# First attention of a two-layer transformer: scores as split fp32r products, normalisation on ScalarE

## The chip, the core and the metric

The kernel runs on one core of a Trainium2 chip. The metric is the device time of one execution in microseconds; the table below gives the median of three runs. A core has TensorE (matmuls, PE in the profile, its weight loads PEld), VectorE (DVE), ScalarE (ACT), GpSimd (POOL) and SyncE (SP, here it only issues transfers). They run side by side and wait for each other by semaphores. Matmul results land in PSUM, eight banks of 512 fp32 columns.

## The reference

Four blocks on x of 4 batches x 512 tokens x 256, each behind a layer norm and added to x: an attention with 16 query and 8 key/value heads of width 128, a mixture of 16 experts, a second attention, and an MLP with ternary weights. The change touches the first attention alone, which is, cut to what matters:

```python
q = rms_norm(einsum('btd,ndh->btnh', x, q_kernel), q_norm_scale)      # 16 heads of 128
k = rms_norm(einsum('bsd,kdh->bskh', x, k_kernel), k_norm_scale)      # 8 heads: 2 query heads share one
v = einsum('bsd,kdh->bskh', x, v_kernel)
q, k = apply_rope(q, positions), apply_rope(k, positions)
mask = (j <= i) & (i - j < 128)                                       # window of 128 tokens
probs = softmax(where(mask, (q * 128**-0.5) @ k.T, -max), axis=-1)
x = x + einsum('btnh,nhd->btd', probs @ v, out_kernel)
```

## The kernel before

Tokens lie in tiles of 128 (4 per batch) and heads in 8 groups of two query heads with their key/value head. A **step** n of a batch is one tile and one group: 32 steps a batch, tile n // 8 outermost, group n % 8 inside. Because the window is 128 tokens, a tile of queries sees two tiles of keys: its own and the one before. In the first 8 steps of a batch (`alone`) there is no older tile.

Each engine has its own written-out `attention_step(b, n, new, old, following)`; batch 0 and batch 3 are unrolled, batches 1 and 2 are passes of a loop on every engine. Within a step an engine works on different stages of up to ten steps (m = n - lag), always in the order of the code; nothing is reordered. The stages and their lags:

- lag 0: PE projects q, q, k, v of the group as one product of 512 columns in high and low parts (six fp32r matmuls, `split_product`, lines 1410 to 1412) into bank 0 or 1; ACT squares (line 1165) and keeps v (1168); DVE reduces (788) and rotates (794, 797, 798); POOL makes the inverse root (526, 528) and adds the rotated halves (530).
- lag 1: DVE scales q and k (777).
- lag 2: PE transposes them into bank 2 (1482); ACT copies all three to `qkT` (1174) and signals `qkT_ready`.
- lag 3: PE computes the scores (1493, 1496) into bank 3 or 4: per head one fp32 product of 128 columns with the older tile's keys and one with its own. An fp32 product is two passes in the trace, so a step with both tiles shows eight at line 1496. Steps without an older tile add the causal mask by a bf16 matmul.
- lag 4: DVE merges older and own scores under the mask into one half of the bank (746) and takes the maximum (768); ACT exponentiates with a row sum (1190) into `prob`, a part of `yT`.
- lag 6: DVE inverts the sums (737) and multiplies the probabilities by them (752), which signals `normed`; PE transposes the result into bank 5 (1525).
- lag 7: ACT copies it (1150); POOL cuts it into the older tile's and the own tile's part (514, 516).
- lag 9: PE multiplies with v (two fp32 products, four passes, line 1454; in steps without an older tile one product, line 1450); ACT and DVE split the result into high and low part (1158, 759).
- lag 10: PE projects it out (six fp32r matmuls of 256 columns, lines 1410 to 1412, `wo`) into bank 7; DVE adds it to x after the eighth group (813).

The order of PE in a step is: attended (lag 9), projection (0), transposes of q and k (2), scores (3), output projection (10), transposes of the probabilities (6). The order of ACT is: copy of the transposed probabilities (7), copy of attended (9), Square and v (0), copy of q and k (2), Exp (4).

At n % 8 == 5 the next tile of x is turned: PE transposes it (`turn_tile`, 1430) into bank 2, the bank of the turned q and k, and therefore waits first for the `qkT_ready` of step n - 2 (line 1502). ACT copies the tile (`tile_keep`, 1123) and DVE makes its low part (`tile_low`, 693). PE wants it in the next step (line 1480). The wait of line 1502:

```python
                if new and (following or n // GROUPS < TT - 1) and n % GROUPS == 5:
                    pe.wait_ge(qkT_ready, k0 + n - 1)
                    turn_tile(b, n // GROUPS + 1)
```

Of the kernel before, what the change touches and what calls it, by code (L numbers as in the profile page):

```python
# [16 lines left out]
ALU = mybir.AluOpType  # L17
# [58 lines left out]
def build(nc, dram, out):  # L76
    with ExitStack() as ctx:
# [40 lines left out]
        qkT = sb("qkT", [P, K_RING, 3, P], where=part_a)  # L118
# [119 lines left out]
        qk_turned, qkT_ready = sem("qk_turned"), sem("qkT_ready")  # L238
# [396 lines left out]
        def _(dve):  # L635
# [92 lines left out]
            def attention_step(b, n, new, old, following):  # L728
# [10 lines left out]
                if valid(m):  # L739

                    k, s = k0 + m, m % 2
                    bank = ps[:, 3 + s, :].rearrange("p (h a f) -> p h a f", h=2, a=2)
                    dve.wait_ge(scored, k + 1)
                    if not alone(m):
                        V.memset(spare[:, 1:2], 0.0)
                        V.copy_predicated(bank[:, :, 1, :], older[:], bank[:, :, 0, :]).then_inc(merged, 1)
                m = n - 6
                if valid(m):

                    k, s = k0 + m, m % 2  # L750
                    dve.wait_ge(inv_ready, k + 1)
                    V.tensor_tensor(prob[:, m % PROB_RING], prob[:, m % PROB_RING],  # L752
                                    rsums[:, s, :].unsqueeze(2).to_broadcast((P, 2, P)), ALU.mult).then_inc(normed, 1)
# [8 lines left out]
                if valid(m):  # L762

                    k, s = k0 + m, m % 2
                    bank = ps[:, 3 + s, :].rearrange("p (h a f) -> p h a f", h=2, a=2)
                    if not alone(m):
                        dve.wait_ge(merged, b * OLDER_STEPS + with_older(m))
                    V.tensor_reduce(nmax[:, s, :], bank[:, :, 1, :], AX.X, ALU.max, negate=True).then_inc(max_ready, 1)  # L768
# [12 lines left out]
                if new:  # L781
# [10 lines left out]
                    if not old and g == 0 and t > 0:  # L792
# [6 lines left out]
                                    ).then_inc(roped, 1)  # L799
                if new and (following or t < TT - 1):  # L800
                    if g == 1:
                        if not old and t in (0, TT - 1):
                            dve.wait_ge(x_loaded[1 + t // (TT - 1)], 16)
                        tile_stats_of(b, t + 1)
                    if g == 3:
                        tile_apply(b, t + 1)
                    if g == 5:
                        tile_low(b, t + 1)
# [301 lines left out]
        def _(act):  # L1110
# [26 lines left out]
            def attention_step(b, n, new, old, following):  # L1137
# [32 lines left out]
                if valid(m):  # L1170
# [3 lines left out]
                    A(qkT[:, m % K_RING, :, :], ps[:, 2, 0:3 * P].rearrange("p (h f) -> p h f", h=3), ACT.Copy  # L1174
                      ).then_inc(qkT_ready, 1)
                if new and (following or t < TT - 1) and g == 5:
                    tile_keep(b, t + 1)
                m = n - 4
                if valid(m):
# [7 lines left out]
                    if old or m >= PROB_RING:  # L1187
                        act.wait_ge(prob_turned, k - PROB_RING + 1)
                    for h in range(2):
                        ins = A(prob[:, m % PROB_RING, h, :], ps[:, 3 + s, (2 * h + 1) * P:(2 * h + 2) * P], ACT.Exp,  # L1190
# [214 lines left out]
        def _(pe):  # L1405
# [29 lines left out]
            def attention_step(b, n, new, old, following):  # L1435
# [49 lines left out]
                if valid(m):  # L1485
# [6 lines left out]
                    if alone(m):  # L1492
                        MM(bank[:, :, 1, :], ident_b[:], causal[:], start=True, stop=False, skip_group_check=True)
                    for h in range(2):
                        for part in ((1,) if alone(m) else (0, 1)):
                            ins = MM(bank[:, h, part, :], qkT[:, m % K_RING, h, :],  # L1496
                                     qkT[:, (m if part else m - GROUPS) % K_RING, 2, :],
                                     start=not alone(m) and h == 0 and part == 0,
                                     stop=h == 1 and part == 1, skip_group_check=True)
# [450 lines left out]
```

## Time and profile before

| | |
|---|---|
| median of 3 runs (lowest to highest) | 1417.8 us (1417.02 to 1418.81) |
| profiled execution | 1424.85 us |
| its span, first to last instruction | 1423.1 us |
| granted TensorE clock, mean | 0.97 |
| TensorE, VectorE, ScalarE, GpSimd busy | 96%, 75%, 51%, 33% of the span |

The first attention takes the first 590 us or so, the experts follow until about 1020, then the second attention and the MLP. A busy TensorE is not TensorE at its peak: the durations of matmuls overlap, and the distance between two starts tells what one costs. In rows of the timeline the first number is the start, the second the time taken, x the count of instructions that were put together, and in brackets the idle time before them with what ended it.

### The profile page before, as it was taken

The page shows a single profiled execution, that of the slowest core. Times are in us where ns is not written, and L with a number is a line of the kernel's source. Part 1 is how long each engine was busy: PE and PEld are TensorE (multiplying, and loading weights), DVE is VectorE, ACT ScalarE, POOL GpSimd, SP SyncE. Part 2 cuts the span into 40 slices and gives each one's busy share as a digit, 9 for nine tenths or more (in the row PEclk, how much of TensorE's full clock was granted, in tenths as well). Part 3 has the DMA queues.
Part 4 walks back from the last instruction along what each step waited for, and adds up shares of the span by engine and source line. Part 5 has one row for each costly group of instructions (what it writes and reads, how often), then busy time and mean ns, then how long its engine had stood idle before and what let it go on. Part 6 is the DMA issues. An engine that isn't in the chain of part 4 may idle for free.

```text
span 1423.1 us, 24271 instructions
## 1 busy us (share of the span) xinstructions
PE 1360.6 (96%) x7418; PEld 1050.1 (74%) x7418; DVE 1062.5 (75%) x2480; ACT 729.2 (51%) x1883; POOL 470.0 (33%) x724
## 2 busy tenths in 40 slices
PE   4799999999999999899999999999999999999898
PEld 3589988988898899788878878878874344444476
DVE  6999999989999999577645445545658878777454
ACT  4555565556555655444432232232336676766575
POOL 5766657765776576200000000000004041331100
PEclk9999999999999999999999999999997899999899
DMA  6200000000000000055311211202152333331001
GB/s 185 78 33 1 1 1 2 2 4 1 1 2 1 2 1 1 24 155 155 116 46 62 65 36 60 65 23 102 60 177 104 106 121 123 117 113 59 1 15 45
DMA packets 45824, 80.73 MB, mean 57 GB/s; under 512 B 5672, under 2 KB 13864, under 8 KB 45420
## 3 DMA queue, kind: packets, MB, share of 16 engines
q1 hardware_dynamic: 45420, 79.22, 17.4%
q8 instruction: 57, 0.93, 0.3%
q14 instruction: 59, 0.48, 0.1%
q0 software_dynamic: 288, 0.10, 0.1%
HBM read 64.57 MB, written 15.87 MB: 57 GB/s over the span
## 4 chain that ended last, share of the span: by engine, by line
PE 71%; DVE 14%; POOL 5%; issue 5%; ACT 2%; DMA 1%; DVEq 0%; SPq 0%; ACTq 0%; POOLq 0%
PE ps L1410 14%; PE ps L1412 14%; PE ps L1411 14%; PE ps L1693 5%; PE ps L1732 5%; PE ps L1496 4%; PE ps L1454 3%; DVE qkn L777 2%; DVE ssum L788 2%; POOL rope L530 2%; PE ps L1821 2%; POOL rms L528 2%; PE ps L1843 2%; DVE nmax L768 2%; DVE yT L752 1%
## 5 line engine op out<-in xcount | busy, mean ns | idle before, releaser
L991 DVE TENSOR_REDUCE nm<-ps 128x1 f32<-128x512 f32 x256 | 166.4, 685 | 53.4 <-PE ps L1693 52.9
L1327 ACT ACTIVATE pT<-ps 128x512 f32<-128x512 f32 x256 | 143.1, 598 | 68.3 <-PE ps L1706 66.7
L489 POOL TENSOR_TENSOR ln_rs<-ln_ve,minus_half 128x4 f32<-128x4 f32 x12 | 15.1, 1260 | 446.7 <-DVE ln_ve L651 446.7
L1410 PE MATMUL ps<-xnT_lo,w1moe_hi 128*128 128x512 f32 x400 | 162.4, 406 | 0.0
L1412 PE MATMUL ps<-xnT_hi,w1moe_hi 128*128 128x512 f32 x400 | 160.9, 402 | 0.0
L1411 PE MATMUL ps<-xnT_hi,w1moe_lo 128*128 128x512 f32 x400 | 160.8, 402 | 0.0
L901 DVE TENSOR_TENSOR sg<-ps,sg 128x512 f32<-128x512 f32 x100 | 69.1, 691 | 118.8 <-ACT sg L1255 118.8
L1233 ACT ACTIVATE moe_act_hi<-sg 128x512 fp32r<-128x512 f32 x100 | 63.2, 632 | 151.6 <-DVE sg L913 151.6
L530 POOL TENSOR_TENSOR rope<-rope 128x384 f32<-128x384 f32 x128 | 132.7, 1037 | 0.0
L1410 PE MATMUL ps<-wqkv_lo,xnT_hi 128*128 128x512 f32 x256 | 127.2, 497 | 4.6 <-DVE wqkv_lo L704 2.8
L1496 PE MATMUL ps<-qkT 128*128 128x128 f32 x896 | 121.4, 276 | 0.0
L1255 ACT ACTIVATE sg<-ps 128x512 f32<-128x512 f32 x100 | 59.7, 597 | 119.3 <-PE ps L1412 119.3
L752 DVE TENSOR_TENSOR yT<-yT,rsums 128x256 f32<-128x256 f32 x128 | 115.7, 904 | 3.2
L1706 PE MATMUL ps<-qsm,kst 64*128 64x512 f32 x256 | 113.1, 498 | 2.9 <-ACT pT L1327 2.7
L919 DVE TENSOR_TENSOR moe_act_lo<-sg,moe_act_hi 128x512 fp32r<-128x512 f32 x100 | 69.2, 692 | 62.4 <-ACT moe_act_hi L1233 62.4
L528 POOL TENSOR_TENSOR rms<-msq,minus_half 128x3 f32<-128x3 f32 x128 | 110.6, 864 | 10.0
L1190 ACT ACTIVATE yT<-ps,nmax 128x128 f32<-128x128 f32 x256 | 92.6, 374 | 39.0 <-DVE nmax L768 39.0
L1496 PEld LDWEIGHTS ps<-qkT 128*128 128x128 f32 x896 | 110.7, 192 | 0.5
L1150 ACT ACTIVATE probT<-ps 128x256 f32<-128x256 f32 x128 | 49.3, 385 | 113.9 <-PE ps L1454 57.5
L1693 PE MATMUL ps<-kst,qst 64*128 64x512 f32 x256 | 105.8, 485 | 1.5 <-DVE nm L991 1.5
L1165 ACT ACTIVATE rope<-ps 128x384 f32<-128x384 f32 x128 | 62.9, 491 | 81.6 <-PE ps L1412 81.5
L1454 PE MATMUL ps<-parted,v 128*128 128x256 f32 x384 | 99.8, 383 | 4.3 <-issue 2.1
(207 smaller groups left out, 3596.2 us busy)
## 6 DMA issues: line engine op xcount, KB each, us to landing
c_rows<-comb_rows SPq DMA_DIRECT2D x36, 256.0 KB, 3.3
copies<-qk_hi SPq DMA_DIRECT2D x32, 256.0 KB
qst<-copies SPq DMA_DIRECT2D x32, 256.0 KB, 2.7
kst<-copies SPq DMA_DIRECT2D x32, 256.0 KB, 3.0
yT<-in_w1moe SPq DMA_DIRECT2D x25, 256.0 KB, 2.6
x_res<-in_wqkv SPq DMA_DIRECT2D x8, 512.0 KB, 4.8
copies<-qk_lo SPq DMA_DIRECT2D x16, 256.0 KB
c_rows<-comb_rows SPq DMA_DIRECT2D x16, 224.0 KB, 3.0
```

Of the source, the lines that this page charges most:

```text
L528: nc.gpsimd.tensor_tensor(rms[:, s, :], msq[:, s, :], minus_half[:, 0:3], ALU.pow).then_inc(rms_ready, 1)
L530: nc.gpsimd.tensor_tensor(rope1[:, s, :], rope1[:, s, :], rope2[:, s, :], ALU.add).then_inc(rotated, 1)
L752: V.tensor_tensor(prob[:, m % PROB_RING], prob[:, m % PROB_RING], rsums[:, s, :].unsqueeze(2).to_broadcast((P, 2, P)), ALU.mult).then_inc( ...
L991: V.tensor_reduce(nm1[:, n % 2, t, col:col + 1], ps[:, 1 + s1_slot(p), :], AX.X, ALU.max, negate=True).then_inc(s1_max, 1)
L1327: A(pT1[:, u % 2, 2 * (m % 2) + h, c, :], ps[:, 4 + e % 2, :], ACT.Exp, scale=SCALE1).then_inc(p1_ready, 1)
L1410: MM(out, left[0], right[1], start=first, stop=False)
L1411: MM(out, left[1], right[0], start=False, stop=False)
L1412: return MM(out, left[0], right[0], start=False, stop=last)
L1454: ins = MM(ps[:, 6, 0:2 * P], v0[:, (m if part else m - GROUPS) % V_RING, :], parted[:, r, part].rearrange("p h f -> p (h f)"), start=part ...
L1496: ins = MM(bank[:, h, part, :], qkT[:, m % K_RING, h, :], qkT[:, (m if part else m - GROUPS) % K_RING, 2, :], start=not alone(m) and h == ...
L1693: MM(ps[:, 1 + s1_slot(p), :], qst[rows, n % STACK_RING, t * P:(t + 1) * P], kst[rows, n % STACK_RING, :], start=True, stop=True).then_inc ...
L1706: MM(ps[:, 4 + e % 2, :], kst[rows, m % STACK_RING, c * P:(c + 1) * P], qsm[rows, m % 2, :], start=True, stop=True).then_inc(st_ready, 1)
```

## The change

Queries and keys are kept as high and low fp32r parts instead of one fp32 `qkT`. ScalarE writes the high parts (q: 256 columns, k: 128) and signals a new `qkT_high`; VectorE subtracts them from PSUM and writes the low parts, and it is VectorE that now signals `qkT_ready`. It does so at the end of its step, behind the rotation. ScalarE waits for the scores of two steps back before it writes q, for q now has two slots (k keeps 16). Scores are three fp32r matmuls per head (high times low, low times high, high times high), and both key tiles are the 256 moving columns of one matmul; the bank half that belongs to the own tile now alternates with the tile (`m // GROUPS % 2`), and merge, maximum and Exp follow. In steps without an older tile the three matmuls have 128 columns each.

The multiplication of the probabilities by the inverse sums leaves VectorE (line 752). ScalarE does it instead, as two Copy activations of 128 columns with a scale per partition, placed behind the q and k copies and `tile_keep` and ahead of Exp.

```diff
-        qkT = sb("qkT", [P, K_RING, 3, P], where=part_a)
+        kT = [sb(f"kT_{part}", [P, K_RING, P], F32R, part_a) for part in ("hi", "lo")]
+        qT = [sb(f"qT_{part}", [P, 2, 2 * P], F32R, part_a) for part in ("hi", "lo")]
...
@@ VectorE @@
-                m = n - 6
-                if valid(m):
-
-                    k, s = k0 + m, m % 2
-                    dve.wait_ge(inv_ready, k + 1)
-                    V.tensor_tensor(prob[:, m % PROB_RING], prob[:, m % PROB_RING],
-                                    rsums[:, s, :].unsqueeze(2).to_broadcast((P, 2, P)), ALU.mult).then_inc(normed, 1)
...
                     V.tensor_tensor(o2[:, :, H2:HD0], rh[:, :, 0:H2], sin3[:, t, :, H2:HD0], ALU.mult
                                     ).then_inc(roped, 1)
+                m = n - 2
+                if valid(m):
+
+                    k = k0 + m
+                    dve.wait_ge(qkT_high, k + 1)
+                    V.tensor_tensor(qT[1][:, m % 2, :], ps[:, 2, 0:2 * P], qT[0][:, m % 2, :], ALU.subtract)
+                    V.tensor_tensor(kT[1][:, m % K_RING, :], ps[:, 2, 2 * P:3 * P], kT[0][:, m % K_RING, :], ALU.subtract
+                                    ).then_inc(qkT_ready, 1)
...
@@ ScalarE @@
                     act.wait_ge(qk_turned, k + 1)
-                    A(qkT[:, m % K_RING, :, :], ps[:, 2, 0:3 * P].rearrange("p (h f) -> p h f", h=3), ACT.Copy
-                      ).then_inc(qkT_ready, 1)
+                    if old or m >= 2:
+                        act.wait_ge(scored, k - 1)
+                    A(qT[0][:, m % 2, :], ps[:, 2, 0:2 * P], ACT.Copy)
+                    A(kT[0][:, m % K_RING, :], ps[:, 2, 2 * P:3 * P], ACT.Copy).then_inc(qkT_high, 1)
                 if new and (following or t < TT - 1) and g == 5:
                     tile_keep(b, t + 1)
+                m = n - 6
+                if valid(m):
+
+                    k, s, r = k0 + m, m % 2, m % PROB_RING
+                    act.wait_ge(inv_ready, k + 1)
+                    for h in range(2):
+                        ins = A(prob[:, r, h, :], prob[:, r, h, :], ACT.Copy, scale=rsums[:, s, h:h + 1])
+                    ins.then_inc(normed, 1)
...
@@ TensorE @@
-                        MM(bank[:, :, 1, :], ident_b[:], causal[:], start=True, stop=False, skip_group_check=True)
+                        MM(bank[:, :, 0, :], ident_b[:], causal[:], start=True, stop=False, skip_group_check=True)
                     for h in range(2):
-                        for part in ((1,) if alone(m) else (0, 1)):
-                            ins = MM(bank[:, h, part, :], qkT[:, m % K_RING, h, :],
-                                     qkT[:, (m if part else m - GROUPS) % K_RING, 2, :],
-                                     start=not alone(m) and h == 0 and part == 0,
-                                     stop=h == 1 and part == 1, skip_group_check=True)
+                        out = bank[:, h, 0, :] if alone(m) else bank[:, h]
+                        keys = [x[:, m % GROUPS, :] if alone(m) else x[:, m % GROUPS::GROUPS, :] for x in kT]
+                        for q, key in ((0, 1), (1, 0), (0, 0)):
+                            ins = MM(out, qT[q][:, m % 2, h * P:(h + 1) * P], keys[key],
+                                     start=not alone(m) and h == 0 and (q, key) == (0, 1),
+                                     stop=h == 1 and (q, key) == (0, 0), skip_group_check=True)
```

## Rows read from the trace of the kernel before

**Rows 1.** Part 1 of the page: busy time, share of the span, instructions.
```profile
PE 1360.6 (96%) x7418; PEld 1050.1 (74%) x7418; DVE 1062.5 (75%) x2480; ACT 729.2 (51%) x1883; POOL 470.0 (33%) x724
```

**Rows 2.** Windows view: length, busy PE, PEld, DVE, ACT, POOL, clock, DMA share, GB/s.
```profile
300.87:438.14 137.27, 136.61 (x897) 122.70 (x896) 132.09 (x363) 79.32 (x292) 92.92 (x171) 1.00 0.01 1
```

**Rows 3.** Timeline of ScalarE: the Squares of four steps.
```profile
75.47 0.49 ACT L1165 ACTIVATE rope<-ps 128x384 f32<-128x384 f32 x1 [0.51 <-PE ps L1412]
...
155.06 0.49 ACT L1165 ACTIVATE rope<-ps 128x384 f32<-128x384 f32 x1 [0.68 <-PE ps L1412]
...
305.20 0.49 ACT L1165 ACTIVATE rope<-ps 128x384 f32<-128x384 f32 x1 [0.59 <-PE ps L1412]
...
309.60 0.49 ACT L1165 ACTIVATE rope<-ps 128x384 f32<-128x384 f32 x1 [0.60 <-PE ps L1412]
```

**Rows 4.** Timeline of TensorE in the step of the Square at 305.20.
```profile
305.32 1.06 PE L1496 MATMUL ps<-qkT 128*128 128x128 f32 x8
...
306.34 0.28 PE L1411 MATMUL ps<-wo_hi,enc_lo 128*128 128x256 f32 x1
...
306.93 0.38 PE L1525 MATMUL ps<-ident,yT 128*128 128x128 f32 x2
...
307.14 1.03 PE L1454 MATMUL ps<-parted,v 128*128 128x256 f32 x4
...
L1454 PE MATMUL ps<-parted,v 128*128 128x256 f32 x384 | 99.8, 383 | 4.3 <-issue 2.1
```

**Rows 5.** ScalarE in that step, and two groups of the whole trace.
```profile
305.58 0.27 ACT L1168 ACTIVATE v<-ps 128x128 f32<-128x128 f32 x1
305.74 0.50 ACT L1174 ACTIVATE qkT<-ps 128x384 f32<-128x384 f32 x1
...
L1190 ACT ACTIVATE yT<-ps,nmax 128x128 f32<-128x128 f32 x256 | 92.6, 374 | 39.0 <-DVE nmax L768 39.0
...
L1213 ACT ACTIVATE w2moe_hi<-w_in 128x256 fp32r<-128x256 f32 x25 | 10.1, 405 | 0.0
```

**Rows 6.** VectorE in that step, and all instructions of line 752 (ns min/median/max).
```profile
304.64 0.42 DVE L759 TENSOR_TENSOR enc_lo<-ps,enc_hi 128x256 fp32r<-128x256 f32 x1
...
305.77 0.55 DVE L788 TENSOR_REDUCE ssum<-rope 128x3 f32<-128x384 f32 x1
...
307.09 0.35 DVE L798 TENSOR_TENSOR rope<-ps,sin 128x192 f32<-128x192 f32 x1
307.36 0.42 DVE L675 BATCH_NORM_STATS2 bn_st<-x_res 128x6 f32 x1
...
L752 DVE TENSOR_TENSOR yT<-yT,rsums x128: 410/1032/1208, 41.8 to 587.8; 128x256 f32<-128x256 f32 x128
```

**Rows 7.** Timeline of the step that turns a tile, batch 2, step 5.
```profile
322.13 0.49 ACT L1165 ACTIVATE rope<-ps 128x384 f32<-128x384 f32 x1 [0.60 <-PE ps L1412]
...
322.68 0.50 ACT L1174 ACTIVATE qkT<-ps 128x384 f32<-128x384 f32 x1
...
323.30 0.43 PE L1430 MATMUL ps<-ident,xn 128*128 128x128 f32 x2 [0.32 <-ACT qkT L1174]
...
323.77 0.38 ACT L1123 ACTIVATE xnT_hi<-ps 128x256 fp32r<-128x256 f32 x1 [0.60 <-PE ps L1430]
```

**Rows 8.** Timeline of TensorE: the gate's fp32r matmuls of 16 columns.
```profile
940.05 0.26 PE L1411 MATMUL ps<-gate_hi,xnT_lo 128*128 128x16 f32 x1
940.17 0.26 PE L1412 MATMUL ps<-gate_hi,xnT_hi 128*128 128x16 f32 x1
```

**Rows 9.** Windows view of the start, columns as above.
```profile
24.00:27.00 3.00, 1.10 (x8) 0.90 (x8) 2.97 (x5) 0.95 (x4) 2.94 (x4) 1.00 0.50 123
27.00:30.00 3.00, 2.53 (x6) 1.79 (x6) 2.11 (x5) 0.86 (x1) 2.98 (x4) 0.58 0.35 72
...
33.00:36.00 3.00, 0.70 (x6) 0.43 (x5) 1.59 (x4) 2.30 (x7) 1.91 (x2) 1.00 0.48 154
36.00:39.00 3.00, 2.74 (x14) 1.72 (x12) 2.55 (x5) 1.29 (x5) 2.88 (x3) 1.00 0.06 23
```

More of the change, by code:

```diff
@@ L237, in build @@
         roped, rotated, qk_normed = sem("roped"), sem("rotated"), sem("qk_normed")
-        qk_turned, qkT_ready = sem("qk_turned"), sem("qkT_ready")
+        qk_turned, qkT_high, qkT_ready = sem("qk_turned"), sem("qkT_high"), sem("qkT_ready")
         scored, merged, max_ready, prob_ready = sem("scored"), sem("merged"), sem("max_ready"), sem("prob_ready")
@@ L745, in attention_step @@
                         V.memset(spare[:, 1:2], 0.0)
-                        V.copy_predicated(bank[:, :, 1, :], older[:], bank[:, :, 0, :]).then_inc(merged, 1)
-                m = n - 6
-                if valid(m):
-                    k, s = k0 + m, m % 2
-                    dve.wait_ge(inv_ready, k + 1)
-                    V.tensor_tensor(prob[:, m % PROB_RING], prob[:, m % PROB_RING],
-                                    rsums[:, s, :].unsqueeze(2).to_broadcast((P, 2, P)), ALU.mult).then_inc(normed, 1)
+                        new_at = m // GROUPS % 2
+                        V.copy_predicated(bank[:, :, new_at, :], older[:], bank[:, :, 1 - new_at, :]).then_inc(merged, 1)
                 m = n - 9
@@ L767, in attention_step @@
                         dve.wait_ge(merged, b * OLDER_STEPS + with_older(m))
-                    V.tensor_reduce(nmax[:, s, :], bank[:, :, 1, :], AX.X, ALU.max, negate=True).then_inc(max_ready, 1)
+                    V.tensor_reduce(nmax[:, s, :], bank[:, :, m // GROUPS % 2, :], AX.X, ALU.max, negate=True).then_inc(max_ready, 1)
                 m = n - 1
@@ L1188, in attention_step @@
                         act.wait_ge(prob_turned, k - PROB_RING + 1)
+                    at = m // GROUPS % 2
                     for h in range(2):
-                        ins = A(prob[:, m % PROB_RING, h, :], ps[:, 3 + s, (2 * h + 1) * P:(2 * h + 2) * P], ACT.Exp,
+                        ins = A(prob[:, m % PROB_RING, h, :], ps[:, 3 + s, (2 * h + at) * P:(2 * h + at + 1) * P], ACT.Exp,
                                 bias=nmax[:, s, h:h + 1], accum_out=psums[:, s, h:h + 1])
```

## The prediction

> **What bounds the kernel now.** I read part 1 of the page first: TensorE is busy 96% of the span, VectorE 75%, ScalarE 51% [rows 1]. Cut by stage, the third pass over the first attention (32 steps) takes 137.27 us, and in it TensorE is busy 136.61, VectorE 132.09, ScalarE 79.32 [rows 2]. So two engines are full and ScalarE has room. The reader should see that the room is an average: it says nothing of where in a step ScalarE's answer is awaited. For that I read one step in order of time. A step is counted from the start of ScalarE's Square (line 1165), which follows the last projection matmul; two Squares are 4.40 us apart [rows 3]. TensorE's list after it is: score passes, output projection, probability transpose (line 1525), attended, next projection. Its matmuls follow each other without a gap, so those 4.40 us are TensorE's sum. Only the first attention, some 590 us of the 1423.1, is touched.
>
> **Scores, steps with an older key tile.** Now eight fp32 passes of 128 columns, the first started at 305.32 in a group of 1.06 us that ends with one matmul's latency; the output projection's second matmul starts at 306.34 and the next group at 306.93, 0.59 for five or 0.118 each, so the first began at 306.22: eight passes cost 0.90, 0.112 each [rows 4]. New are six fp32r matmuls of 256 columns, the form of the output projection: 0.70 (0.71 by this rounding). TensorE gains 0.20 and would reach the probability transpose 1.53 us after the Square where it now does at 1.73 (306.93 less 305.20).
>
> **Scores, steps without one** (8 of 32). Now a mask matmul (0.11) and four passes: 0.56. New: the mask and six fp32r matmuls of 128 columns. No row has that form. From below, the gate's fp32r matmuls of 16 columns start 0.11 to 0.12 apart, bound by the weight load [rows 8], so six cost 0.67. From above, the fp32 product of 128 columns is two passes of 0.112, 0.224, six cost 1.34. I take the upper price, for it is the row with the same width and operands. These steps then reach the transpose at 1.53 - 0.70 + 0.11 + 1.34 = 2.28.
>
> **The copies on ScalarE.** The copy of 384 columns becomes one of 256 (0.38) and one of 128 (0.27). ScalarE starts the next instruction 0.11 before one ends (0.49 long, next 0.38 later) [rows 5]. The added wait for the scores of two steps back is over long before.
>
> **Normalisation moved to ScalarE.** This leaves VectorE (one instruction, 0.41 alone but 1.03 in the median, because it meets GpSimd's work [rows 6]) and comes as two ScalarE instructions of 128 columns with a scale read per partition. Price: 0.27 for the plain one, 0.10 for such an operand (374 ns for the Exp of the same width), 0.02 for a source in SBUF (405 ns against 0.38 us at 256 columns): 0.39 each, 0.28 from start to start [rows 5, 7]. What matters is its place: it stood early in VectorE's step, long before TensorE asked; now it stands behind this step's Square, v copy and two key/query copies, and TensorE asks for it in this very step. After the Square: 0.38 (v) + 0.16 + 0.27 + 0.16 + 0.28 starts the second one at 1.25, it ends at 1.64. TensorE starts 0.17 after a release (a ScalarE copy ends at 323.18, the transposes start at 323.30 and take 0.43 instead of 0.38, so 0.05 more) [rows 7]. So the transpose starts at 1.81, not 1.53. From there to the next Square is fixed TensorE work, 309.60 - 306.93 = 2.67 [rows 3, 4]. The new period is a loop through ScalarE: 4.48, against 4.40 now and 4.20 by TensorE alone. The gain is gone and 0.08 more is lost. Queued behind it is only Exp, 0.6 later, whose result is wanted a step later.
>
> The Trainium skill, "ScalarE: Activation LUTs", section "What ACT_TABLE_LOAD costs", has neighbouring instructions overlap by about 93 ns where the rows show 110; by it the four hand-overs after the v copy would make each step some 0.08 longer, about 9 us in all. The measured overlap is used.
>
> **Low parts on VectorE.** Two subtractions behind the rotation: 256 columns 0.42 (line 759, the same form), 128 columns 0.28 (192 take 0.35), 0.62 together with the overlap of 0.08. VectorE loses up to 1.03 and gains 0.62, so it is lighter and makes up for delays. They start when the reduction (0.57 after the Square) and rotation (1.59) are through, at 2.16, and end at 0.34 + 0.28 later: 2.78 [rows 6]. In most steps the key/query signal is wanted after the next projection: over 1 us to spare.
>
> **The step that turns the next tile.** At n % 8 == 5, line 1502 waits for the key/query signal of step n - 2, because the turned tile goes into the same PSUM bank. Until now ScalarE gave it 1.05 after the Square, and TensorE idled 0.32 [rows 7]. Now VectorE gives it at 2.78 in the same step. TensorE idles until 2.95; behind it stand the output projection, and on ScalarE the tile's copy (line 1123, 0.42 after the turn truly starts at 323.35 [rows 7], so 3.37), behind which the normalisation now waits: 3.37 + 0.27 + 0.28 + 0.39 = 4.31, transpose 4.48, next Square 7.15. That is 2.67 more than a normal new step. It happens four times a batch, three in the last.
>
> **The sum for a batch.** Steps 8 to 15 are followed by an attended product of two passes, not four: 2 x 0.217 = 0.43 less (1.03 for four, 0.383 for one [rows 4]). So 17 steps at 4.48 = 76.2; 4 without an older tile, 4.95 (2.28 + 2.67) = 19.8; 3 of both kinds, 4.52 = 13.6; 4 at 4.05 = 16.2; tile steps 3 x 7.15 + 6.72 = 28.2. Together 153.9 against 137.27: +16.6. Batches 1 and 2: +33.2. Batch 3 has one tile step less (-2.67, and now about -0.4): +14.4. Batch 0 from step 13 on, now 79.6 us (75.47 to 155.06 [rows 3]): 6.72 + 2 x 4.05 + 13 x 4.48 + 2 x 7.15 = 87.4, +7.8. Its first 12 steps run at up to 5.6 us with waits of every kind; the added 0.62 on VectorE before its share is taken away, and one tile step, lie partly beside them: +2, between 0 and 6. Draining the last steps adds one subtraction pair and a longer normalisation to a chain of single waits: +1, between 0 and 3. All: +58.4. The profiled execution took 1424.85 (span 1423.1), which gives 1483.3; it is 0.5% above the median of 1417.8, so the predicted median is 1417.8 + 58.4 = 1476.2. With the lower price of 128 columns 7 steps a batch lose 0.47: 1466. A ScalarE chain 0.1 shorter or longer moves it by some 11.
>
> **Rivals.** (a) The clock falls after the long stalls. For: early in the kernel TensorE was busy 1.10 of the 3 us from 24 to 27, and in the next 3 its granted clock was 0.58, the lower level of 1.2 GHz for most of them; against: it was busy only 0.70 of the 3 from 33 to 36, and stayed at 2.4 GHz in these and the next 3 [rows 9]. A stall of 2.1 in otherwise full work is nearer to the second. If it falls, half of a low stretch of 3 us is lost, some 1.4 x 15 = 21 us: 1497. [...]
> (b) ScalarE's chain is short enough (under 1.53) and TensorE stays the bound except in tile steps: 4.20, 4.95, 4.52, 3.77, tile steps 6.54 and 6.11: 145.6 a batch, +8.3; batch 3 +6.4, batch 0 +1.7, ends +3: +27.7, 1445. For: it lacks 0.28 only. Against: each of its terms is a row.
> (c) Faster: TensorE stays the bound in all steps, the tile steps too. It decides itself at two points of one queue order: normalised by 1.53 and low parts by about 0.8 after the Square. With the lower price of 128 columns a batch then takes 132.4 (-4.9), batch 0 -4.6, ends +3: 1401. Against: the rotation that stands ahead of the low parts can't start before the Square ends.
> (d) No difference: the losses of (b) and the gains of (c) cancel.
>
> **How the numbers follow.** Forecast with either price of 128 columns 0.62, (a) 0.18, (b) 0.12, (c) 0.04, (d) 0.04. The likeliest is 1476. The range takes in (b) and (a): 1445 to 1500; what lies outside is (c), (d) and the ends of (a) and (b). A measurement of this kernel tells 0.2%, 3 us, from no change. Faster 0.05, same 0.03, slower 0.92.
>
> **What would show it.** In the profile after, right if: Squares are about 4.48 apart in steps with an older tile; ahead of line 1525's transposes TensorE idles 0.2 to 0.3 and the releaser is the ScalarE normalisation; line 1430's transposes wait some 2 us for VectorE's subtraction, 15 times; VectorE falls from 96% to some 80% of a pass; TensorE's busy time falls while the pass grows. Wrong if the transposes at 1525 start without a wait, if Squares are nearer than 4.3, if tile steps are under 6 us, or if the granted clock in the attention is under 0.95 (then (a)).

## The result and the profile after

| | before | after |
|---|---|---|
| median of the timed runs, us | 1417.4 (1416.8 to 1418.8) | 1477.6 (1474.5 to 1482.5) |
| ratio to before, 95% interval | | 1.0426 (1.0404 to 1.0447) |
| profiled execution / its span, us | 1424.85 / 1423.1 | 1482.46 / 1480.7 |

The kernel is 4.3% slower, 60.2 us. The prediction was 1476.2.

Part 1 of the page of after answers to [rows 1]. TensorE and VectorE both have a smaller share than before, ScalarE a larger one (54%), and the whole is longer: the two engines that were full became less so, and something waits.

```profile
PE 1381.2 (93%) x7290; PEld 1049.5 (71%) x7290; DVE 1035.3 (70%) x2608; ACT 806.1 (54%) x2267; POOL 454.3 (31%) x724
```

The windows view from the first Square of one batch to that of the next (batches 1, 2 and 3, the last up to the last Square; columns as in [rows 2]):

```profile
171.41:333.75 162.34, 149.17 (x865) 127.20 (x864) 125.56 (x398) 98.68 (x388) 89.74 (x173) 0.94 0.01 2
333.75:488.23 154.48, 145.54 (x866) 125.02 (x865) 124.26 (x395) 98.79 (x389) 89.53 (x171) 0.96 0.01 1
488.23:632.23 144.00, 137.19 (x837) 117.74 (x836) 123.01 (x393) 95.23 (x375) 83.28 (x143) 0.99 0.01 1
```

Batch 2 took 137.27 in [rows 2] and takes 154.48. In it TensorE is idle 8.9 us instead of 0.7, and its clock is 0.96: it is also busier in microseconds, though it runs fewer passes, because part of them ran slower. By the last Square (before 570.47, after 632.23) the difference is 61.8 us: +2.8 up to step 13 of batch 0, +9.0 from there to batch 1, then +21.0, +17.2 and +11.7 for batches 1 to 3. The whole spans differ by 57.6, so behind the attention nothing more is lost; a few microseconds either way are what two executions differ by there.

An ordinary step with an older key tile, timeline of after, batch 2. It answers to [rows 3 to 5].

```profile
413.13 0.49 ACT L1168 ACTIVATE rope<-ps 128x384 f32<-128x384 f32 x1 [0.60 <-PE ps L1426]
...
413.17 0.36 PE L1512 MATMUL ps<-kT_lo,qT_hi 128*128 128x256 f32 x1
...
413.97 0.28 PE L1424 MATMUL ps<-wo_lo,enc_hi 128*128 128x256 f32 x1
...
414.09 0.71 ACT L1189 ACTIVATE yT<-yT,rsums 128x128 f32<-128x128 f32 x2
...
414.56 0.28 PE L1426 MATMUL ps<-wo_hi,enc_hi 128*128 128x256 f32 x1
...
414.86 0.44 PE L1540 MATMUL ps<-ident,yT 128*128 128x128 f32 x2
...
417.59 0.49 ACT L1168 ACTIVATE rope<-ps 128x384 f32<-128x384 f32 x1 [0.60 <-PE ps L1426]
```

The output projection's last matmul starts at 414.56, and 0.12 later TensorE could start the probability transposes. They start at 414.86, behind the normalisation, which runs from 0.96 to 1.67 after the Square. The row gives them 0.44 us where they take 0.38 without a wait [rows 4], so the first of them really begins about 0.06 later, at 414.92. That is 0.24 of waiting, though the profile lists no idle time there, because the row of the matmul before it reaches to 414.84. The two Squares are 4.46 apart.

The step that turns a tile, in the same batch (its scores have no older tile). It answers to [rows 7].

```profile
356.42 0.49 ACT L1168 ACTIVATE rope<-ps 128x384 f32<-128x384 f32 x1 [0.60 <-PE ps L1426]
...
356.83 0.28 PE L1512 MATMUL ps<-kT_hi,qT_hi 128*128 128x128 f32 x1
...
356.94 0.27 PE L1512 MATMUL ps<-kT_lo,qT_hi 128*128 128x128 f32 x1
...
357.05 0.28 PE L1512 MATMUL ps<-kT_hi,qT_lo 128*128 128x128 f32 x1
...
357.17 0.27 PE L1512 MATMUL ps<-kT_hi,qT_hi 128*128 128x128 f32 x1
...
358.98 0.28 DVE L801 TENSOR_TENSOR kT_lo<-ps,kT_hi 128x128 fp32r<-128x128 f32 x1
...
359.38 0.43 PE L1444 MATMUL ps<-ident,xn 128*128 128x128 f32 x2 [1.94 <-DVE kT_lo L801]
...
359.85 0.38 ACT L1126 ACTIVATE xnT_hi<-ps 128x256 fp32r<-128x256 f32 x1 [2.33 <-PE ps L1444]
...
360.13 0.68 ACT L1189 ACTIVATE yT<-yT,rsums 128x128 f32<-128x128 f32 x2
...
360.87 0.44 PE L1540 MATMUL ps<-ident,yT 128*128 128x128 f32 x2 [0.34 <-ACT yT L1189]
```

Two things are seen here. Matmuls of 128 fp32r columns start 0.11 apart. And the tile's turn waits for the last subtraction on VectorE, the normalisation stands behind the tile's copy, and TensorE stops a second time. The waits view of TensorE from 75 to 620 us (us in total, times, longest) counts the first of these, 14 of them:

```profile
PE ps L1444 <- DVE kT_lo L801: 26.3, 14, 2.2
PE ps L1540 <- ACT yT L1189: 4.1, 13, 0.4
```

The four tile steps of batch 2, and below them the last of batch 1 (windows from Square to Square):

```profile
356.42:363.61 7.19, 4.91 (x32) 4.14 (x31) 3.80 (x12) 3.42 (x14) 2.94 (x7) 1.00 0.01 2
392.64:400.61 7.97, 5.83 (x29) 4.70 (x28) 4.77 (x15) 3.42 (x13) 2.04 (x3) 0.79 0.01 2
430.99:439.17 8.18, 6.29 (x31) 5.43 (x30) 4.14 (x14) 3.42 (x13) 2.93 (x7) 0.79 0.00 0
470.42:479.17 8.75, 6.51 (x31) 5.27 (x30) 4.76 (x15) 3.42 (x13) 3.04 (x7) 0.80 0.00 0
```
```profile
309.73:318.46 8.73, 6.49 (x31) 5.22 (x30) 4.79 (x15) 3.42 (x14) 3.04 (x7) 0.80 0.00 0
```

With about the same number of matmuls, TensorE is busy 4.91 at clock 1.00 and 6.3 to 6.5 at 0.79 or 0.80 (5.8 in the second row, whose attended product is the short one). Of the 14 tile steps from step 13 of batch 0 on, 5 kept the clock (6.58 to 7.19) and 9 did not (7.97 to 8.80).

### The profile page after: what moved, and what is told of

The parts are those of the page before. It is cut to its first block, busy times and chain, and to the rows that moved or that the text cites. A ratio compares the mean times of both kernels' runs of the same rounds, so it can differ in the third digit from the quotient of the medians.

```text
span 1480.7 us, 24648 instructions
## 1 busy us (share of the span) xinstructions
PE 1381.2 (93%) x7290; PEld 1049.5 (71%) x7290; DVE 1035.3 (70%) x2608; ACT 806.1 (54%) x2267; POOL 454.3 (31%) x724
## 4 chain that ended last, share of the span: by engine, by line
PE 50%; DVE 2%; ACT 2%; issue 1%; ACTq 0%; POOL 0%; DVEq 0%
PE ps L1424 11%; PE ps L1426 10%; PE ps L1425 10%; PE ps L1708 5%; PE ps L1747 5%; PE ps L1836 2%; PE ps L1858 1%; PE ps L1721 1%; PE ps L1733 1%; PE ps L1666 1%; PE ps L1761 1%; DVE nm L994 0%; PE ps L1653 0%; ACT pT L1341 0%; ACT yT L1404 0%
## 5 line engine op out<-in xcount | busy, mean ns | idle before, releaser
L754 DVE TENSOR_TENSOR enc_lo<-ps,enc_hi 128x256 fp32r<-128x256 f32 x128 | 53.8, 421 | 92.1 <-ACT enc_hi L1161 92.1
L1468 PE MATMUL ps<-parted,v 128*128 128x256 f32 x384 | 105.3, 399 | 4.9 <-issue 3.9
L1426 PE MATMUL ps<-wqkv_hi,xnT_hi 128*128 128x512 f32 x256 | 104.3, 408 | 0.0
L1425 PE MATMUL ps<-wqkv_hi,xnT_lo 128*128 128x512 f32 x256 | 104.3, 408 | 0.0
L1708 PEld LDWEIGHTS ps<-kst,qst 64*128 64x128 f32 x256 | 43.4, 195 | 71.3 <-DVE nm L994 53.4
```

Source lines behind the costliest of these rows:

```text
L1425: MM(out, left[1], right[0], start=False, stop=False)
L1426: return MM(out, left[0], right[0], start=False, stop=last)
L1468: ins = MM(ps[:, 6, 0:2 * P], v0[:, (m if part else m - GROUPS) % V_RING, :], parted[:, r, part].rearrange("p h f -> p (h f)"), start=part ...
L1708: MM(ps[:, 1 + s1_slot(p), :], qst[rows, n % STACK_RING, t * P:(t + 1) * P], kst[rows, n % STACK_RING, :], start=True, stop=True).then_inc ...
```

## The experiments

The theory: the loss has two places. In every step the probability transposes wait for the normalisation on ScalarE, since it is queued behind the Square and three copies of the same step; in the tile steps the turn waits for VectorE's subtractions, because the tile shares PSUM bank 2 with the turned queries and keys. The rival for the first is that any ScalarE normalisation is too long, or that the new score passes are not really shorter; for the second, that the stall moves when it is taken away.

**The normalisation ahead of the Square.** The block of lines 1184 to 1190 is moved on ScalarE up to the place just before the wait for the projection, so that it runs while TensorE still projects.

```
+                m = n - 6
+                if valid(m):
+                    k, s, r = k0 + m, m % 2, m % PROB_RING
+                    act.wait_ge(inv_ready, k + 1)
+                    for h in range(2):
+                        ins = A(prob[:, r, h, :], prob[:, r, h, :], ACT.Copy, scale=rsums[:, s, h:h + 1])
+                    ins.then_inc(normed, 1)
                 if new:
                     act.wait_ge(projected, k + 1)
```

> The changed kernel with one move: ScalarE's two normalising instructions stand ahead of the Square instead of behind the query/key copies. Same instructions, same count. Theory (the loss per step is the place in ScalarE's queue): the probability transposes no longer wait, TensorE alone sets the step, Squares 4.20 apart in steps with an older tile instead of 4.46, 3.77 instead of 4.02 behind a short attended product; tile steps keep their stall (6.5 at the full clock). Some 9 us a batch: 1440 to 1446. Rival (ScalarE's added work or VectorE sets the step): Squares stay at 4.4 or more and the time within 5 us of 1477.

Measured: 1446.4 us, ratio 1.0206 (1.0172 to 1.0241), at the upper end of what was expected and 31 us less than the change. The timeline (its Square is line 1176, the normalisation line 1168) of a step:

```profile
399.50 0.69 ACT L1168 ACTIVATE yT<-yT,rsums 128x128 f32<-128x128 f32 x2
...
400.22 0.49 ACT L1176 ACTIVATE rope<-ps 128x384 f32<-128x384 f32 x1
...
401.67 0.24 PEld L1540 LDWEIGHTS ps<-ident,yT 128*128 128x128 f32 x2
...
401.76 0.38 PE L1540 MATMUL ps<-ident,yT 128*128 128x128 f32 x2
```

The transposes begin 1.54 after the Square, as the prediction's 1.53 for TensorE alone had it, without a wait. Steps with an older tile are 4.22 apart, 0.24 less (some come in pairs such as 4.62 and 3.82, with the same mean); those without one 4.29. So the new scores are shorter, and the place of the normalisation, not its length, was the loss. The tile steps still take 6.3 to 6.6 at full clock and 7.8 to 8.3 where it fell.

**The tile's turn moved.** The turn goes from step 5 of 8, behind the scores, to step 6, between the attended product and the projection; the tile's high and low copies on ScalarE and VectorE move to the place behind those of the attended values.

```
-                if new and (following or n // GROUPS < TT - 1) and n % GROUPS == 5:
-                    pe.wait_ge(qkT_ready, k0 + n - 1)
-                    turn_tile(b, n // GROUPS + 1)
...
                     ins.then_inc(attended, 1)
+                if new and (following or n // GROUPS < TT - 1) and n % GROUPS == 6:
+                    pe.wait_ge(qkT_ready, k0 + n - 2)
+                    turn_tile(b, n // GROUPS + 1)
```

> The changed kernel with the turn of the next tile of x moved from step 5 (behind the scores) to step 6 of eight (ahead of the projection), with its copy and its low part: there the low parts of query and key are long written. Normalisation as in the changed kernel. Theory (the tile steps lose 2.5 each to the wait for VectorE's low parts, and 10 of them another 1.2 to 1.6 because the clock falls after it): tile steps 4.7 to 5.0, granted clock 1.00 all through the attention, other steps unchanged at 4.46; time 1477 less about 45: 1428 to 1436. Rival (the clock falls for another reason, the added work as such): the clock still falls to 0.8 in some steps and only about 33 us come back: 1444.

Measured: 1438.3 us, ratio 1.0145 (1.0114 to 1.0176), 39 less than the change and 2 above what was expected. The steps with the turn are now 4.64 to 4.85 long, 5.02 the first of them (batch 0), at clock 1.00 in all 14 places; the others stay at 4.46. One row of its windows view, the first such step of batch 2:

```profile
332.78:337.62 4.84, 4.80 (x30) 3.66 (x28) 3.74 (x12) 3.31 (x13) 3.06 (x7) 1.00 0.00 0
```

**The low parts ahead of the rotation.** Another way to shorten the same wait: VectorE subtracts before lines 789 to 793 instead of behind them, some 1.0 earlier; the turn stays where it is.

```
                                  ).then_inc(summed, 1)
+                m = n - 2
+                if valid(m):
+                    k = k0 + m
+                    dve.wait_ge(qkT_high, k + 1)
+                    V.tensor_tensor(qT[1][:, m % 2, :], ps[:, 2, 0:2 * P], qT[0][:, m % 2, :], ALU.subtract)
+                    V.tensor_tensor(kT[1][:, m % K_RING, :], ps[:, 2, 2 * P:3 * P], ...
                     dve.wait_ge(summed, k + 1)
```

> The changed kernel with VectorE's two subtractions (low parts of query and key) ahead of the rotation instead of behind it; nothing else. Theory (the tile step waits for their place in VectorE's list): the tile's transposes start at about 1.95 after the Square, not 2.95; tile steps of 6.0 at the full clock, fewer of them slow because the idle stretch is 1.1 instead of 2.1 us; other steps unchanged: 1450 to 1463. Rival (the subtractions or the signal themselves are slow): within 5 us of 1477.

Measured: 1455.1 us, ratio 1.0254 (1.0224 to 1.0284), in the expected range. The timeline of the first tile step of batch 2 (its Square starts at 341.95):

```profile
343.43 0.28 DVE L791 TENSOR_TENSOR kT_lo<-ps,kT_hi 128x128 fp32r<-128x128 f32 x1
...
343.62 0.55 DVE L800 TENSOR_TENSOR rope<-ps,cos 128x384 f32<-128x384 f32 x1
...
343.84 0.43 PE L1447 MATMUL ps<-ident,xn 128*128 128x128 f32 x2 [0.87 <-DVE kT_lo L791]
```

The stall is 0.87 instead of 1.94 and the step 6.09 instead of 7.19. Of the 14 tile steps 13 are 5.6 to 6.1 long with stalls of 0.80 to 0.89; the first, in batch 0, still waits 2.03 and takes 6.81. The clock is 1.00 in all 14. In the profiled executions the last Square comes at 605.18 instead of 632.23, 27 us earlier: 13 are stalls (26.3 in the waits view of the change, 13.1 here), 12 the clock that no longer falls, and 1.4 the passage from batch 1 to 2 (10.85 and 9.45).

**The stall filled.** The change as it is, with eight matmuls of 512 columns put between the scores and the wait of the tile's turn. They write a PSUM bank that is free then, and nobody reads their result: TensorE does more, and every wait stays.

```
+                    if valid(n - 9):
+                        pe.wait_ge(enc_split, k0 + n - 8)
+                    for _ in range(8):
+                        MM(ps[:, 6, :], xnT[0][:, 0, 0:P], wqkv[0][:, 0, 0, :], start=True, stop=True,
+                           skip_group_check=True)
                     pe.wait_ge(qkT_ready, k0 + n - 1)
                     turn_tile(b, n // GROUPS + 1)
```

> The changed kernel with more work: in each step that turns a tile TensorE does eight matmuls of 512 columns (1.9 us at the full clock) into a bank that is free at that time, ahead of the wait for the low parts; their result is used by nothing. Theory (the clock falls because TensorE stands still for 2.1 us): all tile steps take 6.6 to 7.2, the granted clock stays 1.00, and the kernel gets faster by 10 to 15 us although it does more: 1462 to 1469. Rival (the clock falls for another reason, or not at all because of the idle time): still a clock of 0.8 in most tile steps and no gain, 1475 or more.

Measured: 1468.1 us (1465.7 to 1472.3), ratio 1.0335 (1.0304 to 1.0366), in the expected range; the change's own interval is 1.0404 to 1.0447. With some 120 matmuls more the kernel is 9 us faster than the change. Timeline of TensorE in the first tile step of batch 2, and windows of it and the next two:

```profile
348.27 2.06 PE L1520 MATMUL ps<-wqkv_hi,xnT_hi 128*128 128x512 f32 x8
350.38 0.43 PE L1444 MATMUL ps<-ident,xn 128*128 128x128 f32 x2
```
```profile
347.36:354.54 7.18, 6.78 (x41) 5.47 (x39) 3.79 (x12) 3.42 (x13) 2.94 (x7) 1.00 0.00 0
384.00:390.68 6.68, 6.26 (x38) 5.04 (x37) 4.22 (x14) 3.42 (x14) 2.05 (x3) 1.00 0.01 2
422.00:429.11 7.11, 6.71 (x41) 5.50 (x40) 4.14 (x14) 3.65 (x15) 2.94 (x7) 1.00 0.01 2
```

The turn starts as late as before, and the first step takes 7.18 against 7.19. But the next two take 6.68 and 7.11 where the change took 7.97 and 8.18: the granted clock is 1.00 in each of the 14. In the profiled executions the last Square comes at 617.68 instead of 632.23. So the fall of the clock belongs to the idle stretch, and what filling gives back is about what the fall cost: the 14 tile steps together are 12.6 shorter than in the change, where the sum below puts 12.1 on the clock; by the medians it is 9.

**Both moves together.** The normalisation ahead of the Square and the later turn.

> Both moves together: normalisation ahead of the Square, tile turned in step 6. Theory: TensorE is the bound everywhere, 4.20 in steps with an older tile, about 133 us a batch where the kernel before needs 137.3: 1397 to 1406, faster than both kernels. Rival (VectorE, whose list ends with the low parts, becomes the bound once TensorE is faster): steps of 4.3 to 4.4 and 1410 to 1420.

Measured: 1416.6 us, ratio 0.9985 (0.997 to 1.0), no more than no difference, and 10 above the expected range. The time lies in the rival's range, but the rival's steps of 4.3 to 4.4 aren't there: those with an older tile are 4.22 apart in the mean. Batch 2 takes 135.99, 1.28 less than before. The sum of its steps shows why it isn't more. Distances 4 to 13 (counted from the batch's first Square, mostly steps without an older tile and those with short attended products) add up to 40.03 in the kernel before and 41.85 here: +1.82. All the others together: -3.10. What I had left out behind the +1.82 was the price of the score passes without an older tile when TensorE is the bound: six fp32r matmuls of 128 columns are longer than four fp32 passes. Two more losses are not explained by that price. The stretch up to step 13 of batch 0 takes 64.5 instead of 61.4, and the next run, with fp32 scores there, keeps it (64.3); what it is stays open. And VectorE is not out of it altogether, for in step 13 of each batch the turn still waits about 1.0 for the low parts:

```profile
PE ps L1444 <- DVE kT_lo L803: 4.6, 7, 1.1
```

**The same with fp32 scores where there is one key tile.** In steps without an older tile the queries and keys are kept in fp32 by one ScalarE copy, as before, and only the low part of the key is subtracted, for later steps.

```
-                    A(qT[0][:, m % 2, :], ps[:, 2, 0:2 * P], ACT.Copy)
+                    if alone(m):
+                        A(qk0[:, m % 2, :, :], ps[:, 2, 0:3 * P].rearrange("p (h f) -> p h f", h=3), ACT.Copy)
+                    else:
+                        A(qT[0][:, m % 2, :], ps[:, 2, 0:2 * P], ACT.Copy)
...
+                        if alone(m):
+                            ins = MM(bank[:, h, 0, :], qk0[:, m % 2, h, :], qk0[:, m % 2, 2, :],
+                                     start=False, stop=h == 1, skip_group_check=True)
+                            continue
```

> Both moves of the run before, and in addition the steps without an older key tile keep queries and keys as fp32 and take their scores in one product of 128 columns per head. Theory (what these steps lose against the kernel before is the work on ScalarE and VectorE of the high and low parts in the step's loop): the steps without an older tile go from 4.29 to about 4.1 us and the short ones from 3.85 to about 3.65, all others stay, about 1.7 us a batch, so 1409 to 1413, below the kernel before as well. Rival (these steps are set by the chain Square, squares' sum, normalisation, transposes, whose length doesn't depend on the form of the scores): the distances stay within 0.05 us and the time within 2 us of 1416.6.

Measured: 1409.5 us (1409.1 to 1412.2), ratio 0.9945 (0.9933 to 0.9958): faster than both kernels, and in the expected range. The steps without an older tile are 4.06 apart; of the three with neither an older tile nor a long attended product the first is 3.63, the next two are 4.28 and 3.41. Distances 4 to 13 of batch 2 now sum to 40.04, as in the kernel before. Against the run before, batches 1 to 3 are shorter by 5.4 us without the passage from batch 1 to 2, close to the 1.7 a batch that was expected. That passage gives 1.8 more (8.41 and 6.59), which the expectation did not hold: the clock fell in it in the run before and not in this one. The timelines of TensorE in one such step, first without and then with this edit:

```profile
312.66 0.31 PE L1515 MATMUL ps<-kT_lo,qT_hi 128*128 128x128 f32 x1
...
313.36 0.33 PE L1424 MATMUL ps<-wo_lo,enc_hi 128*128 128x256 f32 x1
```
```profile
308.75 0.61 PE L1518 MATMUL ps<-qk 128*128 128x128 f32 x4
309.12 0.36 PE L1429 MATMUL ps<-wo_lo,enc_hi 128*128 128x256 f32 x1
```

In both TensorE runs through without a wait. So the expectation hit the size a batch and named the wrong cause: the 0.23 is TensorE's (0.73 from the mask's matmul at 312.63 to the output projection against 0.48 from 308.64), not the copies' and subtractions' on the other engines.

**The normalisation back on VectorE**, in its old place, everything else as in the change.

> The changed kernel with one part undone: the normalisation is VectorE's again, in its old place; scores in high and low parts, low parts on VectorE. Theory (VectorE was as full as TensorE, so the scores' gain needs the normalisation gone from it): VectorE's list grows from 4.4 by 0.62 to about 4.9 a step and sets it: 1470 to 1490. Rival (VectorE has room, TensorE sets the step): 4.20 a step and 1440 to 1446 as with the early normalisation.

Measured: 1488.9 us, ratio 1.05 (1.046 to 1.054), in the expected range for a wrong reason. The ordinary steps are 4.22 apart, set by TensorE, but for a few of 4.3 to 5.0 in each batch: VectorE does carry the normalisation and the subtractions together, nearly without a loss. What is worse is the tile steps, 7.3 to 10.8. Its group of the normalisation on VectorE (334 to 490 us), and the turn of batch 2's first tile (line 1443), whose step runs from 355.65 to 365.17 with clock 0.82:

```profile
L754 DVE TENSOR_TENSOR yT<-yT,rsums 128x256 f32<-128x256 f32 x32 | 16.2, 507 | 0.8
```
```profile
359.89 0.43 PE L1443 MATMUL ps<-ident,xn 128*128 128x128 f32 x2 [2.86 <-DVE kT_lo L808]
```

The instruction takes 507 ns in the mean of batch 2 where it took 928 in the mean of the same batch before (1032 in the median of all [rows 6]). It was long where it met GpSimd: in the trace of before all 80 that took 0.9 us or more lie across GpSimd's addition of the rotated halves (line 530), and of the 20 under 0.45 only one does. It stands elsewhere against that work now.

**VectorE's normalisation with the later turn.**

> Scores and low parts as changed, normalisation by VectorE in its old place, tile turned in step 6. It tells what the run with VectorE's normalisation lost: there the ordinary steps were 4.22 and only the tile steps grew, to 9 to 10.8. Theory (VectorE has room for both, and only the wait of the tile step turned its lateness into time): steps 4.22, tile steps 4.7 to 5.2, total 1408 to 1420, no slower than with the normalisation on ScalarE ahead of the Square. Rival (VectorE is the bound over a batch; the tile steps' stalls were what let it catch up): steps of 4.4 and more appear once the stalls are gone, 1425 or more.

Measured: 1441.8 us, ratio 1.015 (1.012 to 1.0181). The expected 1408 to 1420 missed. The time lies in the rival's range, but its sign, longer ordinary steps once the stalls are gone, isn't there: they stay at 4.22, with the same few exceptions as in the run with the stalls. Those with the turn take 5.5 to 6.7, since VectorE's subtractions of the step before come late even for the later place. With ScalarE's normalisation ahead of the Square the same kernel is 25 us faster (1416.6). So taking the normalisation off VectorE does pay, and most of it lies in waits for this one signal: the two below add up to 24.8, and to 5.5 there. Its waits view of TensorE from 75 to 620:

```profile
PE ps L1443 <- DVE kT_lo L810: 15.8, 14, 1.5
PE ps L1498 <- DVE kT_lo L810: 9.0, 20, 0.9
```

**The kernel before with ScalarE's normalisation alone**, placed behind the copies as in the change; scores and copies are those of before.

> The kernel before with the normalisation alone moved, to the place it has in the changed kernel (ScalarE, behind the copies of query and key); scores stay fp32, one copy of 384 columns, the query/key signal stays ScalarE's. Theory (the loop through ScalarE sets the step whatever the scores cost): the second normalising instruction ends 1.60 after the Square, steps of 4.44 with and without an older tile (4.40 and 4.06 before), 4.0 behind a short attended product, tile steps 5.4 since the tile's copy stands ahead: +5 us a batch, 1432 to 1442. Rival (the loop binds only together with the new copies): within 5 us of the kernel before.

Measured: 1430.6 us, ratio 1.0079 (1.0048 to 1.0109), slower by 12 and just under the expected 1432 to 1442. All ordinary steps are 4.40 apart, those without an older tile too (4.06 before), those with a short attended product 3.97 (3.63 before where there is no older tile either), tile steps 5.3 to 5.4 (4.82), the short one among them 4.9. The windows row of batch 2:

```profile
303.84:445.35 141.51, 138.94 (x897) 123.04 (x896) 106.54 (x333) 96.88 (x357) 89.46 (x172) 1.00 0.01 1
```

This is the loop through ScalarE by itself: a step with a full attended product isn't shorter than 4.40, and the loop costs where TensorE alone would be faster. VectorE's busy time falls from 132.09 [rows 2] to 106.54, by 25.6 for 32 instructions, 0.80 each, and the kernel is slower still.

## Why the prediction was right, and where it was right by luck

**The loop through ScalarE.** Predicted: normalisation from 0.97 to 1.64, transposes at 1.81, next Square at 4.48. Measured: 0.96 to 1.67, transposes at 1.73 in the row and really at 1.79, next Square at 4.46. The 1.81 held the 0.05 by which transposes begin late behind a wait, so it is to be held against 1.79, and the rest of the step from there is 2.67, as predicted. The normalisation ended 0.03 later, the hand-over took 0.12 instead of 0.17. This is no luck: every term is within 0.05. The first experiment shows that the place in ScalarE's queue is the cause of the 0.24 of waiting. The Trainium skill, "ScalarE: Activation LUTs", section "What ACT_TABLE_LOAD costs", has neighbouring instructions overlap by about 93 ns, which by the prediction's estimate would have made the step 4.56. In the step shown above they overlap by 0.11 to 0.14 and the step is 4.46, so the trace doesn't agree.

**Short attended steps.** 4.05 predicted, 4.02 measured.

**Steps without an older tile.** 4.95 predicted, 4.47 measured. This is a mis-sized term: I took 0.224 for each fp32r matmul of 128 columns, since the nearest row had the same width, and it is 0.11, the lower end. With it TensorE would be at the transposes 1.61 after the Square and ScalarE's loop rules here too. Seven steps of 0.47 in three batches: 9.9 us predicted that weren't there.

**Tile steps.** 7.15 and 6.72 predicted; where the clock held, 6.58 to 7.19. The wait of 1.94 stands where it was put, and the second one behind it of 0.34 too. But rival (a), which I held at 0.18, came true in 9 of 14. Over the predicted tile steps batch 0 lost 1.3 by it, batch 1 5.8, batch 2 3.9 and batch 3 1.1, 12.1 in all where rival (a) had charged 21. Its sign, a clock under 0.95 in the attention, would have missed it: the clock is 0.97 from step 13 of batch 0 to the last Square, and only batch 1 by itself is at 0.94. The step that failed is the weighing of [rows 9]: I took the stretch from 33 to 36 us, with 0.70 of 3.00 busy and no fall, to be nearer than the one with a fall. The Trainium skill, "TensorE: Matmul & The Clock Gate", section "HAM oscillation — how this bites in real kernels", describes a kernel in which waits of 3 to 5 us between bursts bring the slow clock back each time. The waits here are shorter, 1.8 to 2.2 us, and in 9 of 14 places the clock fell behind them, in none of them once they were filled.

**The back edge.** From batch 1 to 2 the last distance is 10.85, where the kernel before took 8.46; the sum had nothing for it: +2.4. TensorE is idle 3.9 in it instead of 2.1, in time for which the profile shows no wait, and its clock is 0.74 instead of 0.80. In the experiments this distance lies between 6.3 and 10.1 without a pattern that I could name.

**The sum.** 57.4 was predicted up to the last Square. Less 9.9, plus 12.1, plus 2.4 is 62.0; measured 61.8. The forecast of 1476.2 against 1477.6 is right in the mechanism and in both places. That it is right to 1.4 us is luck: 9.9 too much for the scores of 128 columns and 14.5 too little for the clock and the passage between the batches mostly cancel, and behind the last Square the change is 4.2 shorter where the sum had +1.

**VectorE.** I called it full, and wrote that it falls from 96% to about 80% of a pass; it is 80% (124.26 of 154.48). But it had not been full: its 132 us held an instruction that was stretched from 0.41 to 1.03 where it met GpSimd's work, and with VectorE's normalisation the subtractions came on top of it without lengthening most ordinary steps. Where it matters is one place, the tile's turn.

## What to carry to other kernels

Moving work to the engine with the lowest share costs what the queue in front of it costs: count from the event that opens the step to the moment its reader asks, and if it comes late, look for a place ahead of that event before giving up the move. As written the change cost 60 us. The place of the normalisation was 31 of them with the turn where it was (22 with the turn moved), the turn 39, and with both moved and the scores of one key tile left in fp32 the kernel is 8 us faster than before. How much of these 8 belongs to the scores and how much to the normalisation isn't shown: no run has the kernel before with the normalisation ahead of the Square alone. A signal that a step gives later than before has to be followed to every reader, the rare ones too: one reader in eight steps made over half of the loss. Whether a split in high and low parts pays on TensorE hangs on the width of the moving operand: at 256 columns six matmuls replaced eight passes (4.40 to 4.22 a step), at 128 columns six replaced four and lost 0.23.

## What the runs showed of the hardware

**An idle stretch of about 2 us may cost the clock, and may not.** Two tile steps of the change, in pieces of 1.5 us, the first with and the second without a fall:

```profile
311.23:312.73 1.50, 0.11 (x1) 0.12 (x2) 1.26 (x5) 0.00 (x0) 1.50 (x2) 1.00 0.00 0
312.73:314.23 1.50, 1.15 (x9) 0.94 (x10) 0.72 (x4) 1.14 (x5) 0.30 (x1) 1.00 0.00 0
314.23:315.73 1.50, 1.50 (x7) 1.23 (x7) 0.12 (x1) 0.52 (x4) 0.00 (x0) 0.59 0.00 0
315.73:317.23 1.50, 1.50 (x5) 1.16 (x4) 0.19 (x1) 0.66 (x2) 0.42 (x2) 0.50 0.00 0
```
```profile
357.92:359.42 1.50, 0.04 (x1) 0.04 (x1) 1.33 (x5) 0.00 (x0) 1.46 (x2) 1.00 0.00 0
359.42:360.92 1.50, 1.16 (x9) 0.96 (x9) 0.49 (x2) 1.07 (x4) 0.38 (x1) 1.00 0.00 0
360.92:362.42 1.50, 1.50 (x8) 1.35 (x9) 0.00 (x0) 0.67 (x5) 0.00 (x0) 1.00 0.04 11
```

The stalls are alike (1.89 and 1.94), and TensorE was full before both. The clock fell to 0.50 (1.2 GHz) only in the first, 1.9 us after work had begun again, when TensorE was already full. In the nine falls this delay lies between 0.1 and 1.9 us. The length of the stall doesn't decide: it is 1.77 to 1.94 where the clock held and 1.77 to 2.19 where it fell. What decides stays open. With the low parts first it fell in none of the 14 places (13 stalls of 0.80 to 0.89 and one of 2.03), with the later turn in none either.

**Filling it pays where the clock would fall.** Matmuls whose result nobody reads, put into the stall, made the changed kernel 9 us faster; where the clock had held anyway the step stayed as it was (7.19 and 7.18).

**Matmuls of fp32r below 256 columns are hardly cheaper.** They start 0.12 apart at 256 columns, 0.11 at 128 and 0.12 at 16 [rows 8].

**A busy share can hold another engine's work.** VectorE was busy 132 of 137 us a batch before. With the normalisation taken away it is busy 106.5, 0.80 less for each of 32 instructions that take 0.41 when nothing meets them [rows 6].
